# State-space phase: an outer-product term moved, for four of sixteen states, from VectorE to TensorE

## What is computed

```python
def step(h, ins):
    dt_t, u_t, B_t, C_t = ins
    h = jnp.exp(dt_t[..., None] * A) * h + (dt_t * u_t)[..., None] * B_t[:, None, :]
    y_t = jnp.einsum('bdn,bn->bd', h, C_t)
    return (h, y_t)
...
xdbl = jnp.einsum('bld,ed->ble', u, Wx)
dtr, Bm, Cm = jnp.split(xdbl, [DT_RANK, DT_RANK + D_STATE], axis=-1)
dt = jax.nn.softplus(jnp.einsum('blr,dr->bld', dtr, Wdt) + bdt)
```

## Time and profile before

| | us |
|---|---|
| median of 3 runs (lowest, highest) | 1843.81 (1840.83, 1847.52) |
| the profiled execution, its own time | 1826.05 |
| its span, first to last instruction | 1824.2 |
| of which the state-space units, about | 45 to 1035 |
| busy: PE, PEld | 1289.2, 890.3 |
| busy: DVE, ACT, POOL | 1453.3, 953.1, 991.7 |
| mean granted TensorE clock (1 is 2.4 GHz) | 0.822 |

### The profile page before, as it was taken

One profiled execution on the slowest core, in us unless ns is written; L12 is line 12 of the kernel. 1 busy time (PEld: TensorE's weight loads), 2 busy tenths in 40 slices (PEclk: granted clock), 3 DMA queues, 4 the chain that ended last, 5 costly groups with the idle time before them and its releaser, 6 DMA issues. The chain is left out here.

```text
span 1824.2 us, 27919 instructions
## 1 busy us (share of the span) xinstructions
PE 1289.2 (71%) x8048; PEld 890.3 (49%) x8048; DVE 1453.3 (80%) x2426; ACT 953.1 (52%) x1520; POOL 991.7 (54%) x908
## 2 busy tenths in 40 slices
PE   3666767577567667665776627789889898989743
PEld 1444545355445444453554403345666666656643
DVE  1999999999999999999999716577668686767412
ACT  4556646664665466556655122555555555546411
POOL 1677767776777677777777542014244243432443
PEclk9877877787789678877876557989989898999876
DMA  4122302320221122022202021125365454645762
GB/s 144 41 95 94 117 0 93 116 84 9 116 93 76 41 93 116 4 89 116 93 17 93 0 59 52 56 84 172 121 180 176 140 160 137 194 126 169 213 213 58
DMA packets 114407, 184.87 MB, mean 101 GB/s; under 512 B 10385, under 2 KB 87185, under 8 KB 109969
## 3 DMA queue, kind: packets, MB, share of 16 engines
q1 hardware_dynamic: 110192, 175.15, 28.1%
q0 software_dynamic: 4096, 8.40, 1.7%
HBM read 153.03 MB, written 25.89 MB: 98 GB/s over the span
## 5 line engine op out<-in xcount | busy, mean ns | idle before, releaser
L731 POOL TENSOR_TENSOR hc<-hb,cb 128x512 f32<-128x512 f32 x512 | 653.8, 1295 | 249.4 <-DVE hb L610 213.8
L610 DVE TENSOR_TENSOR_SCAN hb<-da,dbu 128x512 f32<-128x512 f32 x512 | 599.4, 1201 | 5.6 <-DVE stats L635 4.0
L499 ACT ACTIVATE da<-dt,a_neg 128x512 f32<-128x512 f32 x512 | 351.9, 717 | 354.6 <-DVE hb L610 303.3
L331 PE MATMUL yp<-ident,hc 128*128 128x128 f32 x2048 | 356.9, 317 | 65.7 <-POOL hc L731 65.4
L331 PEld LDWEIGHTS yp<-ident,hc 128*128 128x128 f32 x2048 | 296.9, 165 | 174.3 <-POOL hc L731 93.6
L603 DVE TENSOR_TENSOR dbu<-dtu,bp 128x512 f32<-128x512 f32 x512 | 323.6, 676 | 3.4 <-PE bp L319 2.5
L1750 DVE TENSOR_REDUCE mx<-ms 128x1 f32<-128x384 f32 (+3 forms) x352 | 219.2, 638 | 128.4 <-PE ms L1333 126.8
L1623 ACT ACTIVATE pt<-scores,lift 128x512 f32<-128x512 f32 x320 | 216.4, 684 | 180.8 <-PE scores L1374 180.2
L319 PE MATMUL bp<-st,sel 96*128 96x512 bf16 x256 | 116.4, 455 | 155.9 <-DVE dbu L603 153.4
L2084 POOL DMA_INDIRECT xs_scratch<-h2n,posi x64 | 63.5, 992 | 164.6 <-issue 115.0
L285 PE MATMUL wp<-xpad,wu 128*128 128x512 f32 x256 | 136.7, 627 | 22.1 <-ACT xpad L429 15.6
(11 more groups left out here) (215 smaller groups left out, 2077.8 us busy)
## 6 DMA issues: line engine op xcount, KB each, us to landing
cb<-c_scratch SPq DMA_DIRECT2D x16, 3072.0 KB, 12.0
wt<-ffn_w_e SPq DMA_DIRECT2D x120, 384.0 KB, 4.2
cb<-c_scratch SPq DMA_DIRECT2D x16, 1024.0 KB, 4.6
q<-q_scratch SPq DMA_DIRECT2D x96, 96.0 KB
xg<-xs_scratch SPq DMA_DIRECT2D x24, 256.0 KB, 4.2
ys_scratch<-ysb SPq DMA_DIRECT2D x24, 256.0 KB, 2.3
q_scratch<-qp SPq DMA_DIRECT2D x24, 128.0 KB
k<-k_scratch SPq DMA_DIRECT2D x32, 72.0 KB
```

The lines of the kernel that those rows point to most:

```text
L331: last = nc.tensor.matmul(yp[:, c, h * P:(h + 1) * P], src[:, c * P:(c + 1) * P], ident[:, :], is_transpose=True, start=(s < 0 and h == 0 ...
L499: nc.scalar.activation(da[:, s % NDA, :], dt[:, d, h, :], ACT.Exp, scale=a_neg[:, d, h, n:n + 1]).then_inc(da_done, 1)
L610: nc.vector.tensor_tensor_scan(hb[:, s % NHB, :], da[:, s % NDA, :], dbu[:, s % 2, :], 0.0, ALU.mult, ALU.add).then_inc(scan_done, 1)
L731: nc.gpsimd.tensor_tensor(hc[:, s % NHC, :], hb[:, s % NHB, :], cb[:, d, s // 2, :], ALU.mult).then_inc(hc_done, 1)
```

## The change

For states n = 5, 8, 11 and 14 the product dtu * B is no longer made by DVE. dtu of the unit is transposed once (`pe_dtt`, 8 transposes at s = 3, copied by ACT in `act_dtt`); B is also computed with time on the partitions (`pe_bt`, 8 matmuls of 16 columns in the front, at s = 22, copied by `act_bt`); ACT scales the identity matrix by a column of it (`act_diag`, four 128x128 instructions for a state); and PE multiplies four 128x128 blocks of transposed dtu with these diagonals for each half (`pe_fill`, fp32), which gives dtu * B in PSUM. Half 0 goes into the bp bank of the state and half 1 into a dbu bank; the scan reads both there. dt and dtu are held once instead of per direction.

```diff
+BY_PE = (5, 8, 11, 14)
...
-        dt = sb("dt", [P, NDIR, NH2, SEQ])
-        dtu = sb("dtu", [P, NDIR, NH2, SEQ])
+        dt = sb("dt", [P, NH2, SEQ])
+        dtu = sb("dtu", [P, NH2, SEQ])
+        dtt = sb("dtt", [P, TC, DI])
+        bt = sb("bt", [P, NDIR, TC, NS])
+        diag = sb("diag", [P, 2, TC, P])
...
+        def pe_bt(pe, b, d):
+
+            pe.wait_ge(silu_done, count(silu_done, b, 4 * d + 4))
+            for c in range(TC):
+                for h in range(NH2):
+                    last = nc.tensor.matmul(wp[:, 1 - d, c * NS:(c + 1) * NS], u[:, h, c * P:(c + 1) * P],
+                                            wx[:, d, h, 0:NS], start=(h == 0), stop=(h == 1))
+            last.then_inc(bt_ready, 1)
...
+        def pe_fill(pe, b, d, n, h):
+
+            e = BY_PE.index(n)
+            if h == 0:
+                pe.wait_ge(diag_done, count(diag_done, b, TC * (N_PE * d + e + 1)))
+                pe.wait_ge(dtt_done, count(dtt_done, b, 2 * d + 2))
+                pe_bank_free(pe, b, d, n)
+            else:
+                pe.wait_ge(scan_done, count(scan_done, b, STEPS * d + 2 * n - 1))
+            dst = dbu[:, dbu_bank(d, n), :] if h else bp[:, n % 2, :]
+            for c in range(TC):
+                last = nc.tensor.matmul(dst[:, c * P:(c + 1) * P], dtt[:, c, h * P:(h + 1) * P], diag[:, e % 2, c, :],
+                                        start=True, stop=True)
+            last.then_inc(fill_done if h else b_ready, 1)
...
         def pe_dt(pe, b, d, h):
             if h == 0:
+                pe.wait_ge(bt_done, count(bt_done, b, d + 1))
...
             for s in range(STEPS):
                 if s % 2 == 1 and s // 2 + 1 < NS:
-                    pe_b(pe, b, d, s // 2 + 1)
+                    if made_by_pe(s // 2 + 1):
+                        pe_fill(pe, b, d, s // 2 + 1, 0)
+                    else:
+                        pe_b(pe, b, d, s // 2 + 1)
+                if s % 2 == 0 and made_by_pe(s // 2 - 1):
+                    pe_fill(pe, b, d, s // 2 - 1, 1)
...
+                if s == 3:
+                    pe_dtt(pe, b, d)
...
+                    if s == 22:
+                        pe_bt(pe, *front)
...
+        def act_diag(act, b, d, e):
+
+            act.wait_ge(bt_done, count(bt_done, b, d + 1))
+            act.wait_ge(fill_done, count(fill_done, b, N_PE * d + e - 1))
+            for c in range(TC):
+                nc.scalar.activation(diag[:, e % 2, c, :], ident[:, :], ACT.Copy,
+                                     scale=bt[:, d, c, BY_PE[e]:BY_PE[e] + 1]).then_inc(diag_done, 1)
...
             for s in range(STEPS):
                 act_da(act, b, d, s)
+                if s in (8, 9):
+                    act_dtt(act, b, d, s - 8)
+                for e in range(N_PE):
+                    if s == 2 * BY_PE[e] - 1:
+                        act_diag(act, b, d, e)
...
+            elif h == 0:
+                src = bp[:, n % 2, :]
+                dve.wait_ge(b_ready, count(b_ready, b, NS * d + n + 1))
+            else:
+                src = dbu[:, dbu_bank(d, n), :]
+                dve.wait_ge(fill_done, count(fill_done, b, N_PE * d + BY_PE.index(n) + 1))
...
-                if s % 2 == 1 and s + 1 < STEPS:
-                    dve_dbu(dve, b, d, s + 1)
-                    dve_dbu(dve, b, d, s + 2)
+                n, h = s // 2 + 1, s % 2
+                if n < NS and not made_by_pe(n):
+                    if made_by_pe(n - 1):
+                        dve_dbu(dve, b, d, 2 * n + h)
+                    elif h:
+                        dve_dbu(dve, b, d, 2 * n)
+                        dve_dbu(dve, b, d, 2 * n + 1)
```

More of the change, by code:

```diff
@@ L75, in is_first, with made_by_pe, made_by_dve, dbu_banks @@
     return isinstance(b, int) and b == 0
+BY_PE = (5, 8, 11, 14)
+N_PE = len(BY_PE)
+def made_by_pe(n):
+    return n in BY_PE
+def made_by_dve(s):
+    return sum(1 for i in range(s) if not made_by_pe(i // NH2))
+N_DBU = made_by_dve(STEPS)
+def dbu_banks():
+    banks = [0]
+    for n in range(1, NS):
+        banks.append(1 - banks[-1] if made_by_pe(n - 1) else banks[-1])
+    return banks
+DBU_BANK = dbu_banks()
+def dbu_bank(d, n):
+    return DBU_BANK[n] ^ (d * N_PE % 2)
 def mamba_phase(nc, sems, x, x1, cscr, w):
@@ L280, in pe_u @@
                     pe.wait_ge(ygt_done, count(ygt_done, b, 0))
+                    pe.wait_ge(dtt_done, count(dtt_done, b, 2))
                 elif not first:
@@ L304, in pe_xd, with pe_dtt, pe_bank_free @@
             last.then_inc(xd_ready, 1)
+        def pe_bt(pe, b, d):
[5 more added lines that the diff above has]
+            last.then_inc(bt_ready, 1)
+        def pe_dtt(pe, b, d):
+            pe.wait_ge(dt_done, count(dt_done, b, 2 * d + 2))
+            pe.wait_ge(soft_done, count(soft_done, b, 8 * d + 8))
+            for g in range(2):
+                for c in (2 * g, 2 * g + 1):
+                    for h in range(NH2):
+                        at = (c % 2) * DI + h * P
+                        last = nc.tensor.transpose(wp[:, g, at:at + P], dtu[:, h, c * P:(c + 1) * P], ident[:, :])
+                last.then_inc(dtt_ready, 1)
+        def pe_fill(pe, b, d, n, h):
[11 more added lines that the diff above has]
+            last.then_inc(fill_done if h else b_ready, 1)
+        def pe_bank_free(pe, b, d, n):
+            d_, m = (d, n - 2) if n >= 2 else (d - 1, NS + n - 2)
+            if made_by_pe(m):
+                pe.wait_ge(scan_done, count(scan_done, b, STEPS * d_ + 2 * m + 1))
+            else:
+                pe.wait_ge(dbu_done, count(dbu_done, b, N_DBU * d_ + made_by_dve(2 * m + 2)))
         def pe_dt(pe, b, d, h):
             if h == 0:
+                pe.wait_ge(bt_done, count(bt_done, b, d + 1))
                 pe.wait_ge(silu_done, count(silu_done, b, 4 * d + 4))
@@ L317, in pe_b @@
                 pe.wait_ge(xd_done, count(xd_done, b, 4 * d + 3))
-            pe.wait_ge(dbu_done, count(dbu_done, b, STEPS * d + 2 * (n - 1)))
+            pe_bank_free(pe, b, d, n)
             nc.tensor.matmul(bp[:, n % 2, :], sel[:, n, :], st[:, d, :], start=True, stop=True).then_inc(b_ready, 1)
@@ L341, in pe_ygt @@
             elif d:
-                pe.wait_ge(soft_done, count(soft_done, b + 1, 8))
+                pe.wait_ge(dtt_done, count(dtt_done, b + 1, 2))
             else:
-                pe.wait_ge(soft_done, count(soft_done, b, 16))
+                pe.wait_ge(dtt_done, count(dtt_done, b, 4))
             for h in range(NH2):
@@ L408, in _ @@
             pe_xd(pe, 0, 0)
+            pe_bt(pe, 0, 0)
             pe_dt(pe, 0, 0, 0)
@@ L468, in act_xd, with act_bt, act_dtt @@
                 nc.scalar.activation(mid2[:, :], rem[0:32, :], ACT.Copy).then_inc(xd_done, 1)
+        def act_bt(act, b, d):
+            act.wait_ge(bt_ready, count(bt_ready, b, d + 1))
+            act.wait_ge(diag_done, count(diag_done, b, TC * N_PE * (d - 1)))
+            nc.scalar.activation(bt[:, d, :, :], wp[:, 1 - d, 0:TC * NS].rearrange("p (c n) -> p c n", c=TC),
+                                 ACT.Copy).then_inc(bt_done, 1)
+        def act_dtt(act, b, d, g):
+            act.wait_ge(dtt_ready, count(dtt_ready, b, 2 * d + g + 1))
+            act.wait_ge(fill_done, count(fill_done, b, N_PE * d))
+            nc.scalar.activation(dtt[:, 2 * g:2 * g + 2, :], wp[:, g, :].rearrange("p (c n) -> p c n", c=2),
+                                 ACT.Copy).then_inc(dtt_done, 1)
+        def act_diag(act, b, d, e):
[4 more added lines that the diff above has]
+                                     scale=bt[:, d, c, BY_PE[e]:BY_PE[e] + 1]).then_inc(diag_done, 1)
         def act_soft(act, b, d, h, k):
@@ L498, in act_da @@
             act.wait_ge(scan_done, count(scan_done, b, STEPS * d + s + 1 - NDA))
-            nc.scalar.activation(da[:, s % NDA, :], dt[:, d, h, :], ACT.Exp,
+            nc.scalar.activation(da[:, s % NDA, :], dt[:, h, :], ACT.Exp,
                                  scale=a_neg[:, d, h, n:n + 1]).then_inc(da_done, 1)
@@ L522, in act_front @@
                 act_xd(act, b, d, 1 if at == 27 else 3)
+            if at == 27:
+                act_bt(act, b, d)
             if at == STEPS - 1:
```

27 lines of the change are left out of this document (19 added, 8 removed).

## The result

| | before | after |
|---|---|---|
| median (lowest to highest), us | 1845.66 (1840.83 to 1848.1), 4 runs | 1880.42 (1878.6 to 1883.85), 4 runs |
| ratio, 95% interval | | 1.0194 [1.0166, 1.0222] |
| profiled execution, us; its span | 1826.05; 1824.2 | 1879.18; 1877.4 |
| mean granted clock | 0.822 | 0.874 |
| state-space phase, first scan's start to last scan's end | 984.9 | 1018.1 |

The kernel is slower by 34.8 us. The forecast was 15 slower: the sign is right, the size off by more than a factor of two; the time lies above the 1850 to 1872 that carried most of the chance and inside the whole range, 4.6 under its upper end. The two profiled executions differ by 53, but only 33.2 of that lies in the state-space phase.

A forecast was written before the change was run, and what follows sets the result against it. DVE was taken to bound the state-space phase; per unit, waits for PE and clock less 4.7 us saved gave +1.4 (d = 1) or +1.1 (d = 0), in all +15 us: 1859 us, range 1816 to 1885.

The forecast's parts named there:

- Prices: On PE, from the projection's rows: a fill 0.90 us at full clock, the narrow B matmuls 1.8, bounds 0.2 and 1.8.
- the result by that figure, faster by 9: Alternative sum at 81 ns per matmul: fill 0.65, narrow B matmuls 1.3, about -9 us instead of +15.
- Waits: DVE waiting for PE's fills, per unit: scan 17 1.6 (d = 1) or 2.6 (d = 0), scan 23 4.1 or 2.8 us.
- the sum for scan 17: PE's chain to state 8's fill in unit A: ready at 451.22, scan due 447.42, 3.8 late; 2.6 taken for d = 0.
- the lateness of state 5: PE's delay at state 5's fill, given no separate price but counted within the lateness at scan 17.
- Clock: PE resuming before L294 after scan 17: 1 in 4 at half clock, 1.5 us each, 0.4 a unit on average.
- Rival 3: Clock low where it counts, every resumption at half: +41 us, 1885; needs over about one in two; chance 0.15.
- rivals 1, 2 and 4: 1: PE keeps up better, 1816 us, 0.15; 2: PE never waited for, 1768, 0.06; 4: comes out even, 1844, 0.08.
- What the change takes off DVE: Eight multiplies per unit fewer on DVE at 0.59 us each: 4.7 a unit, 75 us in 16 units.
- on DVE's own past. Nothing: DVE's wait on the dbu buffer, held to depend only on DVE's earlier work and priced at nothing.
- POOL does not stand in the way: POOL's 32 products take 41.4 us of a unit of about 62, so POOL would not limit DVE's saving.
- 90 us of waits against 75 saved: State-space phase: DVE idle about 90 us in all before scans awaiting PE's fills, against 75 us of multiplies removed.

The follow-up runs named there:

- pairs: Changed kernel with states 2, 3, 13 and 14 on PE, B's matmuls and dtu's transposes early, half 1 filled one step earlier, multiplies in pairs: 0.9802, median 1810.8 us.
- singles: The kernel with states 2, 3, 13 and 14 on PE, with one multiply behind each scan of a PE state instead of two together: 0.9846.

## Why the prediction was right, and where it was wrong

- **Prices.** A fill took 477.92 - 477.03 = 0.89 (0.90 forecast), bt 476.38 - 474.67 = 1.71 (1.8, between bounds of 0.2 and 1.8). A narrow record of 16 columns took 1.71 / 16 = 0.107, hardly less than 0.89 / 8 = 0.111 for a load with its pass of 128 columns, so the price went with the loads and not with the columns, as the forecast took it. The Trainium skill ("TensorE: Matmul & The Clock Gate", Back-to-back issue gap) gives some 81 ns for a matmul of 128 columns with its load; the measurement of this fp32 form decides, and the result by that figure, faster by 9, was wrong.
- **Waits.** PE resumes 2.81 us after scan 17 in both kernels, all 15 units. Scan 23 starts 12.17 after it (12.0 forecast) where the clock is full. Scans 17 and 11 cost 28.5 against 29.4. What I had put into the sum for scan 17 as the lateness of state 5 shows itself already at scan 11, 11.1 of the 28.5. I misread one condition: the fill of half 1 may begin one scan earlier than I wrote. It changed nothing, since PE is busy at states 8 and 11.
- **Clock.** 1 in 4 at half was forecast, 4 of 15 came, at 1.4 to 1.6 each. Rival 3 needed one in two and did not come; rivals 1, 2 and 4 had PE cheaper or earlier than it is.
- **The step that failed: what the change takes off DVE.** "Eight multiplies of 32 per unit: 8 x 0.59 = 4.7" counted what went and not what became of the ones that stayed. 0.59 is the price of a multiply in a pair. The change puts two multiplies next to each fill state on their own, each behind a scan it waits for: 0.30 a state, 17.1 us in all. I had written of that wait "on DVE's own past. Nothing". So the sum took it at nothing, though the order of instructions showed the two multiplies of state 15 between the scans of state 14. With pairs against singles, all else equal, it measured 10.3 us for two such states a unit.
- **Also missed: dt.** I looked whether dt would wait for softplus, which it doesn't. Its duration was taken as fixed, and POOL was judged by its total alone: "POOL does not stand in the way: 32 x 1.295 = 41.4 us of a unit". But dt's end follows POOL's running product. Before, in unit A (timelines of POOL and of DVE):

```profile
471.21 2.50 POOL L731 TENSOR_TENSOR hc<-hb,cb 128x512 f32<-128x512 f32 x2 [0.60 <-DVE hb L610]
476.08 2.08 POOL L731 TENSOR_TENSOR hc<-hb,cb 128x512 f32<-128x512 f32 x1 [2.37 <-DVE hb L610]
```

```profile
475.85 1.19 DVE L594 TENSOR_TENSOR dtu<-dt,u 128x1024 f32<-128x1024 f32 x1
```

POOL's products end at 473.71 and dt, which begins at 473.26, at 474.79. After, timeline of POOL at the dt shown above:

```profile
489.07 1.26 POOL L871 TENSOR_TENSOR hc<-hb,cb 128x512 f32<-128x512 f32 x1 [0.26 <-DVE hb L746]
492.71 2.08 POOL L871 TENSOR_TENSOR hc<-hb,cb 128x512 f32<-128x512 f32 x1 [2.37 <-DVE hb L746]
```

POOL's product ends at 490.33 and dt at 489.55 + 1.86 = 491.41. Both times that is 1.08 later, and so it is in all 15 units of both kernels; dt alone takes 1.22. The Trainium skill says ("SBUF — State Buffer", Who interferes with whom) that a DVE instruction with two SBUF inputs and a GpSimd instruction that reads SBUF share a pair of ports under an exclusive lock, so that one waits until the other is done. The trace agrees but for 0.14 us by which dt ends earlier than a full wait would have it (1.08 against 1.22). The next product of POOL agrees too: it meets dtu and takes 2.08 instead of 1.27. That could have been read before the run: the earlier trace rows show dt at 1.53, and dtu, of the same size, takes 1.19 in the row above.

Right sign for mostly the right reason, then: 90 us of waits against 75 saved was measured at 85 against 75, and the 22 of DVE's own decide that it is 35 and not 15.

## What to carry to other kernels

Work moved from the engine that bounds to one with slack on average pays only where that engine has slack at that moment: four states cost 1.9% in one place and gain 2.0% in another (1.5% of it with the multiplies as they were). When instructions are taken out of the bounding engine, price the ones that stay in their new order, each that now directly follows what it waits for. And read an elementwise instruction's duration together with what POOL does in that moment.

## What the hardware showed that I had not expected

- A DVE instruction that waits for the one directly ahead starts 0.03 to 0.11 us after its end instead of 0.085 before it. Two of them in a state cost 0.30 us, half of a 128x512 multiply.
- Not only dt, with its two inputs, is held up beside POOL: four 128x128 normalizations took 3.03 instead of 1.20 beside three products of POOL.
- Eight bf16 matmuls in a wait of 2.3 us kept the clock at its upper level in all 15 units, worth 1.6 us per resumption of the phase where bt was late; moving bt by two steps had lost it in all 15.
